# Scaling the softmax probabilities on VectorE in pairs of heads instead of on GpSimd

## The reference

```python
qkv = (x @ Wqkv + bqkv).reshape(B, S, 3, H, Dh)
...
kwin = jnp.concatenate([kp[:, :, :-2], kp[:, :, 1:-1], kp[:, :, 2:]], axis=3)
vwin = jnp.concatenate([vp[:, :, :-2], vp[:, :, 1:-1], vp[:, :, 2:]], axis=3)
scores = jnp.einsum('bhnqd,bhnkd->bhnqk', qb, kwin) * scale
mask = (jnp.abs(kpos - qpos) <= W) & (kpos >= 0) & (kpos < S)
scores = jnp.where(mask[None, None], scores, jnp.float32(-1e+30))
attn = jax.nn.softmax(scores, axis=-1)
out = jnp.einsum('bhnqk,bhnkd->bhnqd', attn, vwin)
...
x = x + out @ Wout + bout + ffn(xn)
```

## Time and profile before

| | |
|---|---|
| median of 3 runs | 2882.3 us (2880.46 to 2883.25) |
| the profiled execution | 2878.27 us, span 2875.8 us |
| busy in the span | PE 2731.2 (95%), ACT 1667.4 (58%), POOL 1496.9 (52%), DVE 1276.2 (44%) |
| mean granted TensorE clock | 0.984 of full speed |

### The profile page before, as it was taken

The page is one execution under the profiler, slowest core; times in us unless marked ns, Lnnn a source line. Parts: engine busy times, 40 slices in busy tenths (PEclk is TensorE's granted clock), DMA queues, the critical chain, the costliest instruction groups (busy, mean ns, idle before and its releaser), DMA issues.

```text
span 2875.8 us, 55762 instructions
## 1 busy us (share of the span) xinstructions
PE 2731.2 (95%) x19728; PEld 2076.6 (72%) x19728; DVE 1276.2 (44%) x3777; ACT 1667.4 (58%) x4261; POOL 1496.9 (52%) x1362
## 2 busy tenths in 40 slices
PE   6999999999999996799999999999999999999997
PEld 4888888888888885567776667676767676767675
DVE  6444444444444442344444444444444444444443
ACT  6333333333333333377777777777777777777775
POOL 0011111111111110278888888888888888888886
PEclk9999999999999998799999999999999999999998
DMA  5222222222222222201111111111111111111010
GB/s 173 65 88 91 78 80 77 76 89 79 73 73 73 78 77 83 66 23 39 38 53 31 38 52 31 55 35 38 53 31 38 53 31 60 31 38 53 31 42 26
DMA packets 189414, 167.93 MB, mean 58 GB/s; under 512 B 11360, under 2 KB 144480, under 8 KB 188688
## 3 DMA queue, kind: packets, MB, share of 16 engines
q1 hardware_dynamic: 189056, 164.93, 18.3%
q0 software_dynamic: 144, 0.17, 0.0%
HBM read 97.95 MB, written 67.11 MB: 57 GB/s over the span
## 4 chain that ended last, share of the span: by engine, by line
PE 20%; ACT 19%; issue 9%; POOL 6%; DVE 5%; DMA 0%; SPq 0%; ACTq 0%; POOLq 0%
ACT probs L989 10%; PE job_ps L1139 9%; PE pT_ps L1222 9%; POOL probs L949 6%; ACT pT L999 5%; DVE probs L1060 2%; DVE k_lo L1083 2%; ACT k_hi L1018 2%; ACT q_hi L1015 2%; ACT oT_hi L1007 1%; DVE sum_rcp L1067 1%; PE job_ps L1258 0%; PE job_ps L1157 0%; PE job_ps L1148 0%; DMA xT_lo<-xT 0%
## 5 line engine op out<-in xcount | busy, mean ns | idle before, releaser
L949 POOL TENSOR_SCALAR probs<-probs,sum_rcp 128x384 f32<-128x384 f32 (+1 forms) x1024 | 1245.6, 1234 | 299.8 <-DVE sum_rcp L1067 299.8
L989 ACT ACTIVATE probs<-probs,neg_max 128x384 f32<-128x384 f32 (+1 forms) x1024 | 633.0, 618 | 179.7 <-DVE neg_max L1060 179.7
L999 ACT COPY pT<-pT_ps 128x384 f32<-128x384 f32 (+1 forms) x1024 | 486.2, 475 | 249.0 <-PE pT_ps L1222 199.2
L1222 PE MATMUL pT_ps<-ident,probs 128*128 128x128 f32 x3040 | 532.6, 284 | 71.3 <-POOL probs L949 67.1
L1222 PEld LDWEIGHTS pT_ps<-ident,probs 128*128 128x128 f32 x3040 | 316.0, 141 | 349.3 <-issue 273.7
L496 ACT ACTIVATE relu<-up_ps,fc_scale 128x512 f32<-128x512 f32 x256 | 176.2, 688 | 655.4 <-PE up_ps L627 655.4
L1060 DVE CUSTOM_DVE_ANT_0 probs<-score_ps,mask 128x384 f32<-128x384 f32 (+1 forms) x1024 | 504.0, 548 | 72.4 <-PE score_ps L1208 69.4
L456 POOL TENSOR_TENSOR f_y<-f_y,part_in 128x512 f32<-128x512 f32 x64 | 87.4, 1396 | 665.1 <-DVE f_y L561 665.1
L570 DVE SCALAR_TENSOR_TENSOR sq<-up_ps,relu 128x512 f32<-128x512 f32 x256 | 176.9, 691 | 530.1 <-ACT relu L496 529.7
L637 PE MATMUL down_ps<-proj_T,sq_hi 128*128 128x512 f32 x1024 | 408.8, 399 | 0.3 <-DVE sq_lo L553 0.2
L639 PE MATMUL down_ps<-proj_T,sq_lo 128*128 128x512 f32 x1024 | 404.3, 395 | 0.0
(11 more groups left out here) (127 smaller groups left out, 4063.0 us busy)
## 6 DMA issues: line engine op xcount, KB each, us to landing
xT_hi<-xT SPq DMA_DIRECT2D x66, 256.0 KB, 3.9
xT_lo<-xT SPq DMA_DIRECT2D x66, 256.0 KB, 4.4
f_x_in<-in_L_attn_x SPq DMA_DIRECT2D x64, 256.0 KB, 3.0
xT<-f_xT_hi SPq DMA_DIRECT2D x64, 256.0 KB, 2.6
xT<-f_xT_lo SPq DMA_DIRECT2D x64, 256.0 KB, 2.8
part_in<-in_L_attn_x SPq DMA_DIRECT2D x64, 256.0 KB, 3.5
partial<-f_y SPq DMA_DIRECT2D x64, 256.0 KB, 2.0
ff_in<-partial SPq DMA_DIRECT2D x64, 256.0 KB, 3.2
```

Of the source, the lines that this page charges most:

```text
L949: nc.gpsimd.tensor_scalar(probs[:, u, cols], probs[:, u, cols], sum_rcp[:, u:u + 1], None, ALU.mult).then_inc(normalised, 1)
L989: nc.scalar.activation(probs[:, u, cols], probs[:, u, cols], ACT.Exp, bias=neg_max[:, u:u + 1], scale=-1.0, accum_out=prob_sum[:, u:u + 1] ...
L999: nc.scalar.copy(pT[:, h, first + seen.start:first + seen.stop, :].rearrange("p w t -> p (w t)"), pT_ps[:, h % 2, seen.start * P:seen.stop ...
L1222: last = nc.tensor.transpose(pT_ps[:, h % 2, w * P:(w + 1) * P], probs[:, u, w * P:(w + 1) * P], ident[:, :])
```

## The change

GpSimd's `normalise` goes away. VectorE's `invert_sums(t, b)` becomes `normalise(t, b)` at the same two places of its list: for each pair of heads it waits for their two exponentials, inverts their two sums, waits for that reciprocal, and scales the two heads in place.

```diff
         @block.gpsimd
         def _(pool):
-            def normalise(t, b):
-                i, _ = where(t)
-                cols = window(i, b)
-                pool.wait_ge(rcp_done, 2 * t + b + 1)
-                for h in range(HC):
-                    u = b * HC + h
-                    nc.gpsimd.tensor_scalar(probs[:, u, cols], probs[:, u, cols], sum_rcp[:, u:u + 1], None, ALU.mult
-                                            ).then_inc(normalised, 1)
-
...
-                if t < STEPS:
-                    normalise(t, 0)
                 if job_a(t) is not None and where(job_a(t))[0] % 2 == 0:
                     copy_keys(job_a(t))
-                if t < STEPS:
-                    normalise(t, 1)
...
-            def invert_sums(t, b):
-                group = slice(b * HC, (b + 1) * HC)
-                dve.wait_ge(exped, 8 * t + HC * (b + 1))
-                nc.vector.reciprocal(sum_rcp[:, group], prob_sum[:, group]).then_inc(rcp_done, 1)
+            def normalise(t, b):
+                i, _ = where(t)
+                cols = window(i, b)
+                for pair in range(2):
+                    first = b * HC + 2 * pair
+                    heads = slice(first, first + 2)
+                    dve.wait_ge(exped, 8 * t + first + 2)
+                    nc.vector.reciprocal(sum_rcp[:, heads], prob_sum[:, heads]).then_inc(rcp_done, 1)
+                    dve.wait_ge(rcp_done, 2 * (2 * t + b) + pair + 1)
+                    for u in range(first, first + 2):
+                        nc.vector.tensor_scalar(probs[:, u, cols], probs[:, u, cols], sum_rcp[:, u:u + 1], None,
+                                                ALU.mult).then_inc(normalised, 1)
...
                     find_max(t, 0)
-                    invert_sums(t, 0)
+                    normalise(t, 0)
...
                 if t < STEPS:
-                    invert_sums(t, 1)
+                    normalise(t, 1)
```

## The result

The changed kernel takes 2696.49 us (median of 4 runs, 2695.01 to 2696.99), the kernel before in the same runs 2881.38 us: a ratio of 0.9358 with a 95% interval of 0.9342 to 0.9374, 184.9 us less. The forecast was 2710 us, in a range of 2672 to 2775, so it lay 13.5 us too high.

What follows compares the result with a forecast made beforehand. GpSimd's scalings, 1.22 us each, were taken to pace TensorE. Steps would fall from 13.04 to a mean of 11.72 us: 169 us over 128 steps plus 3 at the end, giving 2710 us, range 2672 to 2775.

Steps and rivals of the forecast that it cites:

- GpSimd's beat paces TensorE: Attention steps: TensorE's transposes follow GpSimd's pace of 1.22 us for one scaling; a step takes 13.04 us.
- TensorE's own step, 11.50: Attention step on TensorE with the waits for GpSimd taken out: 13.04 less 1.55, called 11.50 us.
- The price of a scaling, 0.42 and a pitch of 0.34: A 128x384 scaling on VectorE takes 0.42 us, and the next operation starts 0.34 us after its start.
- First pair free, second pair twice on the loop, 11.32 and 11.93: ScalarE-VectorE loop: each half's second pair counts, the first costs nothing; 11.32 us a step, 11.93 with an output addition.
- the formula 9.96 + 4p: Length in us of the ScalarE-VectorE loop without an output addition, p being the pitch of one scaling.
- The prediction's 0.16 us: Behind the first half, 0.16 of the second pair's 0.88 us shows before the remainder of queries and keys.
- The output addition: On VectorE in half of the steps: lengthens the loop by 0.61 us; TensorE's first output matmul waits some 0.4 us.
- The sum: Whole stage: 1.32 us by 128 steps is 169 us, 3 more at the end, 172 us off.
- TensorE alone: Rival: late maxima in the output-addition steps are absorbed, all steps take 11.50 us, time 2682 us; chance 0.15.
- The dearer scaling: Rival: a VectorE scaling costs what the maximum costs, 0.55 us, pitch 0.47, time 2765 us; chance 0.10.
- GpSimd in VectorE's way: Rival: each of GpSimd's 64 bias additions holds up a VectorE scaling for 1.28 us, time 2792 us; chance 0.05.
- Slower: Rival: scalings on the loop four times a step make it slower; break-even at a pitch of 0.69 us; chance 0.03.

Runs made afterwards that it cites:

- e1: Changed kernel with VectorE scaling four heads at once behind the fourth exponential (one reciprocal, four scalings) instead of by pairs: 2864.1 us, ratio 0.9946.
- e2: Kernel before, scaling still on GpSimd, but reciprocals and scalings go by pairs of heads behind their exponentials: 2673.2 us, ratio 0.9283.
- e3: Changed kernel with VectorE's output addition moved from ahead of the next step's first maxima to behind them: 2668.6 us, ratio 0.9268.
- e6: Changed kernel without reciprocals and scalings, TensorE waiting for the exponentials (output wrong): 2665.2 us, ratio 0.9261.
- e7: Changed kernel with VectorE scaling head by head, a reciprocal of one sum and one scaling after each exponential: 2665.5 us, ratio 0.9262.
- e4: Changed kernel with two spare VectorE scalings of 128x384 behind each pair, into a tile nobody reads: 2825.7 us, ratio 0.9815.
- e10: Changed kernel with scaling head by head on VectorE and the output addition behind the first maxima, both together: 2673.1 us, ratio 0.9277.
- e5: Changed kernel with GpSimd doing six spare scalings of 128x384 a step beside VectorE's scalings: 2780.6 us, ratio 0.9662.
- e9: Changed kernel with GpSimd filling a 128x384 tile with a constant 16 times a step beside VectorE's scalings: 2739.0 us, ratio 0.9507.

## Why the prediction was right

*GpSimd's beat paces TensorE.* Right as to the place, since the 1.22 is gone with everything else; but e1 and e2 put the cause more sharply than the prediction did. It named GpSimd's pace for one scaling; what made the pace visible was that four scalings started only behind the fourth exponential. GpSimd at the same pace, started by pairs, doesn't hold TensorE up (e2), and VectorE at a third of the time, started by fours, brings 0.5% (e1).

*TensorE's own step, 11.50.* It is 11.43 (short steps of the changed kernel, e3, e6, e7). The scores took the 0.73 of the forecast. Of each four quarters the first took 1.08 to 1.10, the next two 1.02 to 1.04, and the last 1.12 where 1.15 was counted.

*The price of a scaling, 0.42 and a pitch of 0.34.* Measured 0.418 and 0.33. The 0.26 by the Trainium skill ("VectorE: DVE Perf Modes", section on the TRN2 errata) didn't come true; the two rows of the preparation were the better guide. (From 512 to 384 columns they go back by 128 and not by the prediction's 256; its 0.42 is right.)

*First pair free, second pair twice on the loop, 11.32 and 11.93.* 11.30 (through e4) and 11.86 to 11.89. e1 and e4 moved the loop by what the formula 9.96 + 4p says: with four more of 0.27 the long step rose by 1.08 (e4), with four more of 0.33 by 1.35 (e1, 11.88 to 13.23). The prediction's 0.16 us that show at the remainder are 0.14 (0.17 behind ScalarE's operation, 0.03 before).

*The output addition.* Long steps are long because of it alone (e3). TensorE's wait at its first output matmul was forecast at 0.4; it is 0.32 there (0.63 less 0.31). With it this quarter is 0.35 to 0.38 longer than in a short step, and most of the rest of the 0.45 stands two quarters later.

*The sum.* The time came out 13.5 us below the forecast. In the profiled executions the span fell by 181.7: the first five steps gave 11.5 (63.4 to 51.9 us), the 119 of the steady state 1.383 each, 164.5, three behind them 2.3, the last step with the end 3.0, and what lies before the first scores 0.3. The forecast had 172: 1.32 for every step and 3 for the end. So 0.063 too little in the mean step makes 7.5 us, the first five steps gave 4.9 more than forecast, and the last four with the end 2.9 less. Another 3.6 us come from the median, which lay 4.0 us above the profiled execution before and only 0.5 above it in the changed kernel.

The 4.9 us go with the granted clock. From 1210 to 1240 us the kernel before ran at 0.77 of full speed in the mean; from 1215 to 1220 it was 0.52 and from 1230 to 1235 0.50, about the lower of the clock's two levels (1.2 GHz), and in the 5 us before either of them TensorE had work in hand for 3.55. Its third and fourth steps took 14.1 and 14.5 us. The changed kernel ran at 1.00 there, and these steps took 10.3 and 11.0. e1 ran at 0.77 there too (14.4 and 14.8 us, where its short steps later take 12.6), while e3, e6, e7 and e10 ran at 1.00 and none of their first five steps is longer than their later ones. No run changes the clock alone.

*The rivals.* TensorE alone (2682) needed the maxima to catch up; they don't until the addition is moved. The dearer scaling (2765) failed on the scaling's row, 0.418 us. GpSimd in VectorE's way (2792) is a true mechanism, e3, e5, e9 and e10 show it, and its price in e5 is 84 us (88 by the ratios); it doesn't strike in the changed kernel because of where the bias addition stands (2004.84 to 2006.13, no scaling due), as the prediction said, and it strikes as soon as the addition moves. The Trainium skill ("SBUF — State Buffer", section "SBUF: two separate sides") has the mechanism right, and for the bias addition and the fills the size too: a scaling was held until 0.22 us behind their end. GpSimd's scalings held one VectorE scaling to their end and let another through before it, which a lock for the whole of a recorded instruction doesn't explain. *Slower* needed a scaling that adds 0.69, and it adds 0.33. *No change* needed a falling clock, and from 1290 to 1811 us it was 1.00 before and after.

## What to carry to other kernels

Ask first what an operation waits for, and only then which engine does it: starting after two inputs instead of four was worth 206 us on the slow engine, and the fast engine without it 15. With it, the fast engine was 22 us slower than the slow one, because its queue was on the loop. An operation in a queue costs what it adds behind the last input that it waits for, so a small group of work directly behind its own producer is nearly free, and the same work behind the last one is paid in full, twice a step here. When one wait is gone, look at what stands behind the work that took its place: 0.6 us of an addition at the head of a queue cost 26 to 28 us, and moving it can bring two engines into each other's way.

## What the runs showed of the hardware

A VectorE multiplication of 128x384 float32 from SBUF to SBUF takes 0.42 us alone. Beside GpSimd it is held until a GpSimd operation is over: in e3, e9 and e10 every longer one (60, 609 and 60 in 119 steps) ends 0.21 to 0.23 us behind the end of a GpSimd addition or fill, wherever it started. So its length says only how much of the GpSimd operation was left: 1.48 us behind a bias addition that had started 0.02 us before (e10), 0.75 behind one that had started 0.75 us before (e5), 0.65 beside a fill of 0.42 to 0.51 (e9), and 1.81 when the bias addition and the fill behind it passed first (e9).

GpSimd's multiplication of 128x384 by a constant (1.17 us) is the exception: in e5 it held some scalings to its end and let others through 0.45 us before it. The recorded ends of GpSimd's operations are rough, and why this one differs is left open.

GpSimd gave way less: its bias addition took 1.29 us in e10 and 1.35 in the mean of e9, against 1.28 before; a fill took 0.46 in the mean, against 0.41 for the one that prepares the mask before. VectorE's maximum, which reads PSUM and one SBUF operand, stayed at 0.55 throughout.
